# Stacking query and key rows with copies inside on-chip memory, and new step places, in a one-core decoder layer

## What is computed

```python
x1 = layernorm(x + gated_projection(x))
x2 = layernorm(attention(query=x1 + pos, key=ctx + pos, value=ctx + pos) @ Wo + x1)
x4 = layernorm(x1 + layernorm(relu(x2 @ W1 + b1) @ W2 + b2 + x2))
qkv = x4 @ in_proj_w.T + in_proj_b                  # second attention, 16 heads, softmax over 256 keys
x5 = layernorm(attention(qkv) @ out_proj_w.T + x4)  # then the router's logits
```

## Time and profile before

| | us |
|---|---|
| median of 3 runs | 1010.25 (1004.7 to 1012.99) |
| the profiled execution | 1008.04 |
| its span, first to last instruction | 1006.1 |
| gate stage, up to the first scores | 118.55 |
| sixteen attentions, first scores to the last context | 118.55 to 788.24 |
| the rest, mixture of experts | to 1006.1 |
| PE busy over the span | 681.6 (68%) |
| DVE busy over the span | 516.7 (51%) |
| ACT busy over the span | 260.9 (26%) |

### The profile page before, as it was taken

How to read it: one execution, slowest core, us unless ns; L and a number is a source line. 1 busy time by engine, 2 the same in 40 slices (tenths; PEclk the granted TensorE clock), 3 DMA queues, 4 the chain that set the end, 5 groups by cost and what they waited for, 6 DMA issues and landing times. The chain is left out here.

```text
span 1006.1 us, 12601 instructions
## 1 busy us (share of the span) xinstructions
PE 681.6 (68%) x4120; PEld 452.7 (45%) x4121; DVE 516.7 (51%) x1231; ACT 260.9 (26%) x382; POOL 167.2 (17%) x172
## 2 busy tenths in 40 slices
PE   5844487676977868688885967977668551999500
PEld 4723254443644445355553544544434320787400
DVE  3874235353654635356364454544535283555276
ACT  2101040313324222142240413413132260222102
POOL 3003310102201102020120202101010035000063
PEclk9976687978989879797797978969796655999855
DMA  5555331505224051433213334223140092222323
GB/s 214 159 177 203 90 80 28 136 13 147 65 53 117 25 122 33 115 96 69 69 60 89 85 83 97 66 53 80 37 116 12 19 311 83 62 64 68 110 69 99
DMA packets 58989, 92.51 MB, mean 92 GB/s; under 512 B 7665, under 2 KB 46005, under 8 KB 55481
## 3 DMA queue, kind: packets, MB, share of 16 engines
q1 hardware_dynamic: 52650, 79.39, 29.2%
q0 software_dynamic: 1680, 7.21, 2.1%
q10 hardware_dynamic: 4608, 5.24, 1.5%
HBM read 58.01 MB, written 33.29 MB: 91 GB/s over the span
## 5 line engine op out<-in xcount | busy, mean ns | idle before, releaser
L1351 DVE TENSOR_REDUCE a_nmax<-wide 128x4 f32<-128x1024 f32 x128 | 153.0, 1218 | 150.7 <-PE wide L981 150.5
L981 PE MATMUL wide<-a_K,a_Q 48*128 48x256 f32 x512 | 74.0, 394 | 103.2 <-DMA a_Q<-pack_d 98.5
L1193 ACT ACTIVATE a_E<-wide 128x1024 f32<-128x1024 f32 x128 | 125.0, 1015 | 46.1 <-PE wide L981 46.1
L863 POOL TENSOR_TENSOR a_rstd<-a_var,nhalf 128x2 f32<-128x2 f32 x40 | 27.9, 698 | 580.5 <-DVE a_var L1316 580.5
L1172 ACT ACTIVATE a_th<-bank 128x512 f32<-128x512 f32 x48 | 28.7, 598 | 367.9 <-PE bank L928 367.9
L981 PEld LDWEIGHTS wide<-a_K,a_Q 48*128 48x128 f32 x512 | 49.7, 248 | 139.1 <-issue 128.0
L134 PE MATMUL bank<-a_th,dw 128*128 128x256 f32 x320 | 94.2, 445 | 6.3 <-ACT a_th L1172 6.2
L134 PE MATMUL bank<-dw,a_th 128*128 128x256 f32 x320 | 98.2, 436 | 0.0
L134 PEld LDWEIGHTS bank<-dw,a_th 128*128 128x128 f32 x320 | 66.5, 219 | 34.0 <-issue 20.6
L134 PEld LDWEIGHTS bank<-a_th,dw 128*128 128x128 f32 x320 | 66.2, 217 | 26.0 <-ACT a_th L1172 14.7
L981 PE MATMUL wide<-a_Q,a_K 50*128 50x256 f32 x512 | 63.5, 332 | 20.8 <-ACT a_E L1193 20.0
(11 more groups left out here) (262 smaller groups left out, 1103.2 us busy)
## 6 DMA issues: line engine op xcount, KB each, us to landing
pack_d<-a_stage SPq DMA_DIRECT2D x64, 256.0 KB, 2.4
a_K<-pack_d SPq DMA_DIRECT2D x32, 256.0 KB, 4.5
a_Q<-pack_d SPq DMA_DIRECT2D x32, 256.0 KB, 4.2
w<-in_w_dram SPq DMA_DIRECT2D x1, 4096.0 KB
a_K<-pack_d SPq DMA_DIRECT2D x32, 128.0 KB, 3.5
a_Q<-pack_d SPq DMA_DIRECT2D x32, 128.0 KB, 4.8
x_d<-a_x SPq DMA_DIRECT2D x16, 256.0 KB, 4.7
m_w<-in_w_dram SPq DMA_DIRECT2D x1, 4096.0 KB, 21.1
```

The costliest lines, as they stand in the source:

```text
L863: pool.tensor_tensor(rstd[l][:, :], var[l][:, :], nhalf[:, 0:T], ALU.pow).then_inc(rs_ok[l].s, 1)
L981: last = pe.matmul(pW[r % 2][:, c * 512 + e * S:c * 512 + (e + 1) * S], left[l][part_, s, tok(t)], right[l][part_, s, :], start=True, stop ...
L1193: act.activation(Ex[g % 2][:, kt, :, :], pW[r % 2][:, :].rearrange("p (h s) -> p h s", h=4), ACT.Exp, scale=HD ** -0.5).then_inc(ex.s, 1)
L1351: dve.tensor_reduce(nmax[l][:, t, :].rearrange("p (h c q e) -> p h q c e", h=HALVES, c=C, q=2)[:, jj // 2, jj % 2, :, :], pW[r % 2][:, :]. ...
```

## The change

`stack` no longer goes through device memory. It waits for the high part, issues four copies (two row blocks for each half) straight from `a_stage` to the tile, then waits for each low part and issues one copy for each half. All six copies of a stack are of 16 rows, 128 KB each, cut in pieces of 1 KB; before it was two writes of 256 KB, two reads of 256 KB and two of 128 KB. The semaphores of the write are gone, and `heads_hi` waits for the copies of the attention before instead. `stack_k` waits for the ones of the key tile only in its first call. The five tables of places are new. The other edits (slices in place of `bass.ds` with the same constants, one chain object on DVE in place of a list with one) leave the instructions as they were.

```diff
-            def stack(i, l, a, x_, lo0, lo, w, r, tile, parts):
-
+            def stack(i, l, a, x_, hi, lo0, lo, r, tile, hi_rows, lo_row):
+
+                sp.wait_ge(cx_tr[l].s, cx_tr[l].at(i, a - 1))
+                sp.wait_ge(hi[l].s, hi[l].at(i, a))
+                for c in range(C):
+                    for row in hi_rows:
+                        sp.dma_start(tile[l][64 * c + row:64 * c + row + HD, :, :].bitcast(F32),
+                                     stage[l][:, x_, c, 0, :].bitcast(F32)).then_inc(r[c][l].s, 16)
                 for c in range(C):
                     if c == 0:
                         sp.wait_ge(lo0[l].s, lo0[l].at(i, a))
                     else:
                         sp.wait_ge(lo[l].s, lo[l].at(i, a))
-                    sp.wait_ge(r[c][l].s, r[c][l].at(i, a - 1))
-                    sp.dma_start(pack_d[l, x_, c].rearrange("m p t -> p m t"), stage[l][:, x_, c, :, :].bitcast(F32)
-                                 ).then_inc(w[c][l].s, 16)
-
-                sp.wait_ge(cx_tr[l].s, cx_tr[l].at(i, a - 1))
-                for c in range(C):
-                    sp.wait_ge(w[c][l].s, w[c][l].at(i, a))
-                    for row, m, lo_, hi_ in parts:
-                        sp.dma_start(tile[l][64 * c + row:64 * c + row + m, :, :].bitcast(F32),
-                                     pack_d[l, x_, c, lo_:hi_].rearrange("m (d s) t -> (m d) s t", s=HC)
-                                     ).then_inc(r[c][l].s, 16)
+                    sp.dma_start(tile[l][64 * c + lo_row:64 * c + lo_row + HD, :, :].bitcast(F32),
+                                 stage[l][:, x_, c, 1, :].bitcast(F32)).then_inc(r[c][l].s, 16)
...
 AT_PE = {
...
-    "middle": {0: 1.5, 2: 3.5, 3: 4.25, 6: 5.5, 8: 6, 9: 6.25, 11: 8.5, 12: 9.5, 16: 13.25, 18: 14.45, 19: 14.5, 21: 14.95, 22: 14.95, 24: 15.95, 25: 16.45},
+    "middle": {0: 0, 2: 0, 3: 0, 6: 1, 8: 3, 9: 4.25, 11: 6.25, 12: 7, 16: 14.95, 18: 16.95, 19: 16.95, 21: 16.95, 22: 16.95, 24: 16.95, 25: 16.95},
```

More of the change, by code:

```diff
@@ L116, in build @@
         attention_stage(nc, I, sem, ident, nhalf, chan, wtok, logit, dw, w1, ahead, pT, pD, pW,
-                        vT_d, pack_d, x4_d, x5_d)
+                        vT_d, x4_d, x5_d)
         next_stage()
@@ L591 @@
     "tail": {},
-    "middle": {4: 3.25, 5: 4.5, 13: 6.75, 14: 11.25, 15: 13.95},
-    "last": {4: 4},
-    "first": {0: 2, 8: 9, 9: 16.95},
+    "middle": {4: 1.75, 5: 6.75, 13: 8.45, 14: 10.25, 15: 11.25},
+    "last": {4: 2.45},
+    "first": {0: 1.75, 8: 11.7, 9: 14.45},
 }
 AT_SP = {
-    "own": {0: 3.5, 1: 8.5},
+    "own": {0: 0.5, 1: 12.75},
     "tail": {},
-    "middle": {4: 11, 20: 11.45, 23: 12.25, 26: 16.45},
-    "last": {5: 8.5},
-    "first": {5: 4.25, 14: 8.95},
+    "middle": {4: 0, 20: 15.2, 23: 16.7, 26: 16.95},
+    "last": {5: 8},
+    "first": {5: 8.45, 14: 15.2},
 }
@@ L619, in attention_stage @@
 def attention_stage(nc, I, sem, ident, nhalf, chan, wtok, logit, dw, w1, ahead, pT, pD, pW,
[L620 removed]
+                    vT_d, x4_d, x5_d):
     with ExitStack() as ctx:
@@ L657, in attention_stage @@
         cin_in, x_in, vT_in = lane("cin_in", 1, 16), lane("x_in", 1, 16), lane("vT_in", 1, 16)
-        q_w, k_w = ([lane(f"{n}{c}", 2, 16) for c in range(C)] for n in ("q_w", "k_w"))
-        q_r, k_r = ([lane(f"{n}{c}", 2, 32) for c in range(C)] for n in ("q_r", "k_r"))
+        q_r, k_r = ([lane(f"{n}{c}", 2, 48) for c in range(C)] for n in ("q_r", "k_r"))
         max_r = [lane(f"max_r{h}", 2, 64) for h in range(HALVES)]
@@ L680, in attention_stage, with walk @@
         dch = one("dch")
-        PAIR_CHAIN = 24
         block = ctx.enter_context(nc.Block())
-        def walk(eng, at, attention, own, tail, first, middle, last, region=None):
+        def walk(eng, at, attention, own, tail, first, middle, last):
             def beside(*parts):
@@ L714, in walk @@
             attention(0, 0, 0, beside(("own", own, (0, 0, 0)), ("first", first, (0, 1))))
[L715 to L719, removed]
+            for i in range(PAIRS):
+                pair(i, i < PAIRS - 1)
             for n in range(TAIL):
@@ L1446, in last @@
                     dve.wait_ge(mm_r[l].s, mm_r[l].at(i, 0))
-                    dve.tensor_tensor(logit[:, bass.ds((2 * i + l) * T, T), :],
+                    dve.tensor_tensor(logit[:, (2 * i + l) * T:(2 * i + l + 1) * T, :],
                                       pD[l][:, 0:T * 12].rearrange("p (t n) -> p t n", t=T),
                                       brow[:, :].unsqueeze(1).to_broadcast([P, T, 12]), AD).then_inc(lg_ok[l].s, 1)
-            walk(dve, AT_DVE, attention, own, tail, first, middle, last, region)
+            walk(dve, AT_DVE, attention, own, tail, first, middle, last)
 GROUP = 2 * T
```

68 lines of the change are left out of this document (30 added, 38 removed).

## The result

The changed kernel takes 1052.66 us (median of 4 runs, 1048.33 to 1055.93) against 1007.49 us for the kernel before on the same chip. The ratio is 1.0439, with a 95% interval of 1.037 to 1.0507: slower by 45 us. The profiled execution, the quickest of the four, has a span of 1046.6 us.

A forecast was written before the change was run, and what follows sets the result against it. Bound by a chain through one lane, with holes from stacking and order. Middle slots 45.6, turn slots 13.2, first and last attention 4.4, first stacking 3.8: 67.0 off 1008.0, 941.0 profiled, 943 us median; range 920 to 976.

The forecast's parts named there:

- the 1.0 us allowed in a turn slot: Turn slot: 1.0 us added for maxima rows queued behind the keys' copies and for queries, making 35.2 us against 37.4.
- a gain of 2.2: First and last attention: half of the turn-slot steps stand beside them, so each gains 2.2 us, 4.4 together.
- work at 1.2 GHz in middle slots only: Middle slot: W_1 at a low clock after a PE idle gap adds 1.2 us, giving 41.0 against 46.7.
- 4.9 us a stack at 157 GB/s: Stacking copies: 768 KB at the old reads' rate, so 6.3 us from high part to scores instead of 10.1.
- the 0.43 taken from reads: SP's issue of stacking copies: 0.43 us each, as for the old reads, so 2.6 us for six.
- The first stacking of all: Stacking ahead of the very first scores: gains 3.8 us.
- Rival 1: Stacking: 16-row copies are each as slow as a read, 7.5 us for six; +32 us, 975 us; chance 0.17.
- the estimate of 7.2 us a stack: Stacking: 16 partitions reach only 4 of 16 ports, about 109 GB/s; counter-evidence the forecast set aside for 4.9 us.
- the walk: Attention slots stepped through under the new places: middle slot 41.0 us against 46.7, turn slot 35.2 against 37.4.
- Rival 3: Slower: copies so slow that next scores wait longer than places save; at 11 us a stack about 1047 us; chance 0.04.
- Rival 2: Middle chain loses more to places than walked: 3 us per middle slot, 0.5 per turn slot; +27, 970 us; chance 0.14.
- rival 4: No change: the wait for queries becomes PE's wait for the norm ahead of first scores; 1000 us; chance 0.04.

The follow-up runs named there:

- e4: Changed kernel with the keys' copies of a turn slot moved from place 8.45 to 12.9 on SP's queue, behind the second maxima rows: 992.6 us.
- e10: Changed kernel with four useless PE matmuls in each of the seven waits for the second maxima rows, which land as late as before: 1015.4 us.
- e6: Changed kernel with all stacking copies left out after the first of each lane, waits and steps kept: 929.0 us.
- e7: e4 with two to five useless PE matmuls ahead of the wait for queries at the head of each slot but the first: 954.6 us.
- e3: e4 with the queries' copies sent to a separate tile of all 128 partitions, same pieces and bytes: 930.1 us.
- e11: e4 with each stack's two high copies into the lower half of the tile issued from ACT's queue: 985.6 us.

## Why the prediction was wrong

**The step that failed most: the 1.0 us allowed in a turn slot** for maxima rows that queue behind the keys' copies and for queries. The mechanism was named, its size was not worked out. In each of the seven slots with the wait it is 3.2 us of wait and 3.6 us of slow clock (e4, e10): 6.9 in place of 1.0, together 48 of the 55 us by which the profiled executions of the changed kernel and of e4 differ (60 by medians). One of the seven is the first slot, for which the forecast had no allowance but a gain of 2.2; it lost 4.2. I had walked the keys' copies as work with time to spare, which they have, and not asked who stands behind them on SP's queue. A price for the queue was at hand: by the forecast's own numbers a stack of six copies takes 6.3 us from first issue to landing, so a row right behind them could be late by up to that. And I had counted work at 1.2 GHz in middle slots only (1.2 us each), though the earlier trace rows show it behind an idle of 2.44 us (0.74 in W_1's stretch), shorter than a row could be late.

**Second: 4.9 us a stack at 157 GB/s.** It is 116 GB/s, and an issue is 0.64 us (2.57 for four), not the 0.43 taken from reads. A nearer row was there: the maxima rows of before, also transfers inside of on-chip memory, take 0.57 us to issue (the row has ns least/median/most, then first and last start in us); I priced the issue by reads from device memory instead.

```profile
L788 SPq DMA_DIRECT2D a_Q<-a_mrow x128: 572/573/710, 128.1 to 773.7; - x128
```

A stack became 9.2 us from high part to scores in place of 6.3 in a turn slot; in a middle slot keys and queries together land 8.3 us after the context, not 3.2. The first stacking of all, counted with 3.8, gave 0.3 (first scores at 118.27 in place of 118.55). Rival 1 with 7.5 us a stack was close. So was the estimate of 7.2 us a stack worked out from the Trainium skill (SBUF — State Buffer, Door 1: the DMA port swizzle), with which the trace agrees: 768 KB at 116 GB/s are 6.8 us. With rows first, copies as they are give 992.6, and without them 929.0: 64 us for copies, and some 7 more without e6's first slot, of which the forecast carried next to nothing. Rival 1 gave +32 for this; it left out the clock behind the waits, which in e7 is 38 us. By medians the forecast's miss is the sum of the two: 60 for the rows' place and 64 for the copies, less 14 by which the walk was too slow, make the 110 between 943 and 1052.7.

**Right: the places.** Walked 41.0 and 34.2 us (35.2 less the allowance); e6 gives 40.8 and 32.6. The steps inside are off, the sum is not, and that their errors cancel so well is luck: in e6 x2 is ready 6.5 us after the context (walked 7.1), the norm behind W_2 starts at 23.4 (20.3), x4 ends at 29.2 (26.0), and the next context comes at 42.6 in a middle slot that is followed by another. With copies that cost nothing the walk would have been some 14 us too slow (21 without e6's first slot), in the main by its allowance and by turn slots 1.6 us shorter than walked.

**The other edits** left the instructions as they were, as said: PE has 4120 in both kernels, DVE 1231.

**Rivals.** Rival 3 (slower) had the right sign and nearly the right time, 1047 us, by the wrong mechanism: it needed 9.6 us a stack for the next scores' wait (9.3 if the sum is redone with only the three waits that are over zero there), while the loss came in a wait for other transfers, with stacks of 7.9 us in the same count (9.2 from high part to scores, less the 1.0 and 0.3 at its ends). Its nearness in time is luck. Rival 2 (places) fell in e6, rival 4 with it. The chance of 0.04 for slower came from asking only how slow a stack must be to be late itself.

By medians, then: 1052.7 less 37 (PE kept busy in the rows' wait, of which 25 are shown in its slots), less 23 (the wait itself), less 38 (PE kept busy at the head waits) is e7's 954.6; a further 25 us goes if the queries' copies aren't into 16 partitions (930.1 in e3, which has no work of no use in it). The last two overlap: with quick copies the head waits behind the first are 0 to 2.2 us, and little is left to fill.

## To carry to other kernels

When a transfer is moved on a queue, ask who stands behind it there, and price the wait for the smallest transfer with the nearest deadline: here 4 KB rows behind 768 KB of copies that nobody needed yet cost 60 us, three times the 20 that the change gives without it, and one number mended it. An idle of 3 to 4 us on PE in a dense stretch must be priced with the stretch at 1.2 GHz behind it, which here cost at least as much as the idle (3.6 us a slot against 3.2). Transfers into few partitions want their own row for the price, from a destination of the same shape.

## What was not expected of the hardware

- Work of no use in PE's waits made the kernel it was added to faster: 37 us (e10, 7 waits of 3.7 to 3.95 us) and 38 us (e7, 15 waits of 1.2 to 5.8 us), by medians. Behind an idle of 3.94 us the granted clock was 0.50 for 9 us; with the idle filled it was 1.00.
- A 1 KB piece took a transfer engine 164 ns into 16 partitions and 48 ns into 128 (e4, e3, worked out from share and GB/s); a second queue raised 116 to 127 GB/s only (e11).
- Issuing one of the copies from on-chip to on-chip memory takes SP 0.62 to 0.64 us in the timelines shown, a read from device memory 0.43 to 0.55.
